# Image 0's key rotations on VectorE, and a different order of the work around the first projections, in a fused vision-transformer layer

## The chip, the cores and the metric

The kernel runs on one core of one Trainium2 chip. The metric is the device time of one launch in microseconds. Five engines work side by side, each on its own instruction list: TensorE (PE; its weight loads are shown apart as PEld), VectorE (DVE), ScalarE (ACT), GpSimd (POOL), and SyncE (SP), which issues the DMAs. They meet only at semaphores: an instruction waits for a count that others raise.

## The reference

32 images of 256x256 are filtered and then go through one transformer layer of 257 tokens (a class token and 256 rows) by 256 features. Cut to what matters:

```python
cur = img
for _ in range(3): cur, h, v, d = _dwt2(cur); details.append((h, v, d))
aw = sigmoid(cur.reshape(B, -1) @ Wa + ba)                  # one gate per image
w = softmax(flat(h, v, d) @ Wd + bd)                        # three gates per level and image
rec = idwt2(rec, h * w[0], v * w[1], d * w[2])              # rebuilt level by level
h = concat([cls_tok, rec])
h = h + attention(layernorm(h))     # 16 heads of 64, rotary q and k, alibi bias, causal
h = h + ffn(layernorm(h))           # ternary weights, 8-bit activations, silu gate
# rotary: q * cos + rotate_half(q) * sin, the same for k
# ternary: clip(round(w / mean|w|), -1, 1)
```

## The kernel before

**Start.** All images' gates are found first. TensorE multiplies the whole input by a map of ten bands (`zbank`, 128 products in four quarters `q`, one per landed quarter `xs[q]`), VectorE and ScalarE make softmax and sigmoid of the sums, TensorE spreads them to all partitions (`bcast_ready`), and VectorE turns them into small row operators, `image_operators(i, n)` for n images from i on. Meanwhile the feed-forward weights become ternary: `ternary(k, part)` on VectorE, three passes over 2048 columns for each of gate, up and down (k = 0, 1, 2; the "signs"); `turn_weights(w)` transposes them on TensorE (the "turnings"), and ScalarE copies each bank out (twice for each w). The quantiser's mean comes from one small product of TensorE ("mean product", into `psum[1]`).

**Each image a** then passes these stages. GpSimd makes its row operators (`row_operators`), TensorE filters it (`coarse`, `synthesise`), VectorE adds the parts (`image_out`) and takes the layernorm statistics (`image_stats`, `normalise_image`), TensorE transposes it (`turn_input`), ScalarE and VectorE split it into two fp16 halves (`input_hi`, `input_lo`). `project(b, g)`, g = 0 to 7, gives the queries (even g) and keys (odd g) two head pairs at a time in one PSUM bank; ScalarE's `to_rotate` copies each to `rq` (count `rq_ready`); SyncE moves it across partitions to `rot` by DMA (`rot_done`); GpSimd's `rotate(b, g)` multiplies `rq` by cos (`pcos_done`), `rot` by sin (`t2_ready`) and adds them (`qk_done`). Then come four value projections `project_v(b, v)` in the same bank, each read by ScalarE (`values_hi`) and VectorE (`values_lo`, count `vl_done`), and `project_v(b, v + 1)` waits for `values_lo(b, v)`. Then scores, softmax, output and the feed-forward part follow, interleaved with the next image.

**What sets the order** is the code itself. Every engine has a prologue written out by hand, and then a function `step(s)` run for every s from -4 on, which lists that engine's pieces for images s - 3 to s + 2; pieces whose image doesn't exist do nothing. Image 0's first pieces stand in the prologues. On GpSimd image 0's order is `add_bias(0)` (which adds the output bias `ob` and waits for VectorE's copy of it, `ob_copied`), rotations 0, 1 and 2, `row_operators(1)`, rotations 3, 4, 5, `image_rstd(1)`, rotations 6 and 7, `add_bias(1)`. On TensorE `project(0, 5)` stands behind the filtering of image 1. `out_bias` folds the class token's values into the output bias with float32 products, and `ob_ready` follows its last.

## Time and profile before

| | |
|---|---|
| median of 3 runs | 1754.96 us (1750.04 to 1756.24) |
| the profiled execution | 1752.32 us, its span 1750.5 us |
| busy share of the span | PE 95%, PEld 73%, DVE 84%, ACT 76%, POOL 64% |
| end of the start-up: `project_v(0, 3)` of image 0 done, its first scores | about 131 us |
| mean granted clock of TensorE | 0.976 of full speed |

The span is from the first to the last instruction. Busy shares are averages over the span; the change touches only the first 135 us of it, where TensorE is busy less (the profile's first three slices of 44 us show 7, 7 and 5 tenths). That stretch has to be read instruction by instruction.

### The profile page before, as it was taken

What the parts mean: (1) busy time and instruction counts of PE and PEld (TensorE: products, weight loads), DVE (VectorE), ACT (ScalarE), POOL (GpSimd) and SP (SyncE); (2) the same over time, 40 slices, a digit from 0 to 9 for tenths busy, and PEclk for the clock granted to TensorE, in tenths of its full rate; (3) what the DMA queues carried; (4) which work ended last, traced back from release to release, by engine and by line L of the source; (5) the groups of instructions that cost most, each with busy time, mean ns of one, the idle gap of its engine ahead of it and who ended that gap; (6) DMA issues with size and microseconds to landing.
All of it is one profiled execution on the core that took longest, in us unless ns stands there. A gap on an engine that the chain in (4) does not pass through costs nothing.

```text
span 1750.5 us, 48653 instructions
## 1 busy us (share of the span) xinstructions
PE 1664.2 (95%) x16742; PEld 1278.3 (73%) x16742; DVE 1470.0 (84%) x4972; ACT 1323.6 (76%) x3812; POOL 1120.1 (64%) x1034
## 2 busy tenths in 40 slices
PE   7758999999999999999999999999999999999975
PEld 6635777777777777777777777777777777777653
DVE  3837888899888888899888888899888888889874
ACT  0326888888888888888888888888888888888762
POOL 0087667766777666766777667666677667666500
PEclk9789999999999999999999999999999999999986
DMA  9311111111111111111111111111111111111100
GB/s 320 110 61 61 56 53 56 53 67 57 61 68 68 59 61 57 50 65 62 56 68 68 66 55 60 54 56 66 55 64 68 68 53 61 56 53 62 44 7 13
DMA packets 90168, 113.70 MB, mean 65 GB/s; under 512 B 14818, under 2 KB 52163, under 8 KB 89667
## 3 DMA queue, kind: packets, MB, share of 16 engines
q1 hardware_dynamic: 89922, 110.59, 18.1%
q8 instruction: 135, 2.21, 0.5%
q14 instruction: 111, 0.90, 0.2%
HBM read 26.62 MB, written 8.42 MB: 20 GB/s over the span
## 4 chain that ended last, share of the span: by engine, by line
PE 88%; DVE 4%; SPq 3%; POOL 2%; ACT 1%; issue 1%; DMA 0%; DVEq 0%; POOLq 0%; ACTq 0%
PE bank L725 45%; PE bank L842 9%; PE bank L983 7%; PE bank L831 6%; PE bank L829 6%; PE bank L994 3%; PE bank L853 3%; PE bank L903 3%; PE bank L891 2%; PE bank L1003 2%; SPq L320 1%; PE bank L882 1%; DVE arena L1283 1%; PE bank L950 0%; POOL rot L486 0%
## 5 line engine op out<-in xcount | busy, mean ns | idle before, releaser
L482 POOL TENSOR_TENSOR arena<-rq,cos 128x512 f32<-128x512 f32 x256 | 326.1, 1274 | 280.0 <-ACT rq L526 280.0
L535 ACT ACTIVATE arena<-arena,nm 128x129 f32<-128x129 f32 (+1 forms) x1024 | 455.6, 455 | 0.0
L486 POOL TENSOR_TENSOR rot<-rot,sin 128x512 f32<-128x512 f32 x256 | 326.3, 1275 | 103.9 <-DMA rot<-rq 103.9
L725 PE MATMUL bank<-xt_h,weights 128*128 128x256 f16 x2048 | 378.9, 273 | 9.2 <-ACT rq L526 7.8
L526 ACT ACTIVATE rq<-bank,bqk 128x256 f32<-128x256 f32 x512 | 214.4, 471 | 170.1 <-PE bank L725 155.3
L1283 DVE CUSTOM_DVE_ANT_0 arena<-bank,bias 128x129 f32<-128x129 f32 (+1 forms) x1024 | 317.9, 352 | 26.5 <-issue 16.6
L489 POOL TENSOR_TENSOR arena<-arena,rot 128x512 f32<-128x512 f32 x256 | 314.2, 1228 | 37.3 <-POOL rot L486 0.9
L1291 DVE TENSOR_TENSOR ptr_l<-bank,ptr_h 128x384 f16<-128x384 f32 x512 | 280.0, 552 | 31.8 <-ACT ptr_h L545 29.4
L545 ACT ACTIVATE ptr_h<-bank 128x384 f16<-128x384 f32 x512 | 249.1, 486 | 68.6 <-PE bank L725 44.0
L725 PE MATMUL bank<-xt_l,weights 128*128 128x256 f16 x1024 | 279.6, 273 | 0.0
L842 PE MATMUL bank<-eye,arena 128*128 128x128 f32 x1536 | 253.0, 277 | 8.5 <-DVE ptr_l L1291 4.4
L725 PEld LDWEIGHTS bank<-xt_h,weights 128*128 128x128 f16 x2048 | 200.5, 98 | 54.4 <-ACT rq L526 19.9
L842 PEld LDWEIGHTS bank<-eye,arena 128*128 128x128 f32 x1536 | 178.2, 141 | 43.8 <-issue 20.0
L535 ACT ACTIVATION_READ_ACCUMULATOR arena<-arena,nm 128x1 f32 x1024 | 203.9, 199 | 0.0
L725 PEld LDWEIGHTS bank<-arena,ptr_h 128*128 128x128 f16 x3072 | 175.7, 98 | 23.3 <-DVE ptr_l L1291 10.9
L725 PE MATMUL bank<-arena,ptr_h 128*128 128x64 f16 x3072 | 191.1, 193 | 0.1
L725 PE MATMUL bank<-arena,ptr_l 128*128 128x64 f16 x1536 | 178.9, 193 | 0.0
L725 PE MATMUL bank<-weights,arena 128*128 128x256 f16 x1536 | 178.5, 273 | 0.0
L725 PEld LDWEIGHTS bank<-weights,arena 128*128 128x128 f16 x1536 | 148.4, 98 | 16.6
L725 PE MATMUL bank<-weights,xt_h 128*128 128x512 f16 x512 | 152.7, 380 | 5.3 <-DVE arena L1404 4.2
L831 PE MATMUL bank<-arena 64*128 64x257 f32 x1024 | 155.1, 380 | 0.0
L983 PE MATMUL bank<-wgu,xqt 128*128 128x512 f16 x528 | 141.2, 390 | 5.1 <-ACT q2t L526 2.3
(200 smaller groups left out, 3182.5 us busy)
## 6 DMA issues: line engine op xcount, KB each, us to landing
rot<-rq SPq DMA_DIRECT2D x512, 128.0 KB, 2.0
arena<-in_x SPq DMA_DIRECT2D x4, 2048.0 KB, 15.2
xin<-in_x SPq DMA_DIRECT2D x32, 256.0 KB, 2.8
hr<-hr SPq DMA_DIRECT2D x32, 256.0 KB, 2.3
out<-h SPq DMA_DIRECT2D x64, 128.0 KB, 2.1
arena<-in_L_attn_w_qkv SPq DMA_DIRECT2D x2, 1536.0 KB, 8.6
weights<-in_L_ffn_w_down SPq DMA_DIRECT2D x1, 1024.0 KB, 11.8
arena<-in_L_ffn_w_gate SPq DMA_DIRECT2D x1, 1024.0 KB, 8.5
```

Of the source, the lines that this page charges most:

```text
L482: pool.tensor_tensor(dst, rq[:, g % 2].rearrange("p j (t n) -> p j t n", t=T), cos[:, :].rearrange("p (t n) -> p t n", t=T).unsqueeze(1).b ...
L486: pool.tensor_tensor(r, r, sin[:, :].unsqueeze(1).broadcast_to([P, 2, SIDE]), ALU.mult).then_inc(t2_ready, 1)
L489: pool.tensor_tensor(dst, dst, r.rearrange("p j (t n) -> p j t n", t=T), ALU.add).then_inc(qk_done, 1)
L526: return act.activation(dst, src, ACT.Identity, **kw)
L535: act.activation(cols, cols, ACT.Exp, bias=nm[:, t, h:h + 1], scale=-1.0, accum_out=rs[:, t, h:h + 1]).then_inc(e_done, 1)
L545: act.activation(ptr_h[:, h % PTR_RING], pt_bank[u % 2][:, 0:3 * P].rearrange("p (b n) -> p b n", b=3), ACT.Copy).then_inc(hi_done, 1)
L725: ins = pe.matmul(dst, lhs[l], rhs[r], start=start and n == 0, stop=stop and n == len(parts) - 1)
L831: pe.matmul(bank[:, W0:SCOLS], qt[par][half, j, P:SIDE], kt[par][half, j, :], start=True, stop=True).then_inc(s_ready, 1)
L842: ins = pe.transpose(pt_bank[u % 2][:, n * P:(n + 1) * P], r[:, col:col + P], eye[:, :])
L983: ins = pe.matmul(bank[:, :], xqt[:, kc, t * P:(t + 1) * P], wgu[:, kc, base + half * 512:base + (half + 1) * 512], start=kc == 0, stop=kc ...
L1283: dve.tensor_tensor_reduce(r[:, cols], bank[:, cols], b, -1.0, 3.0e38, ALU.add, ALU.min, nm[:, t, h:h + 1]).then_inc(t_done, 1)
L1291: tt(ptr_l[:, h % PTR_RING], pt_bank[u % 2][:, 0:3 * P].rearrange("p (b n) -> p b n", b=3), ptr_h[:, h % PTR_RING], ALU.subtract).then_inc ...
```

## The change

In words, engine by engine, all before the steady state:

- **TensorE**: the mean product moves from behind quarter 2 of the band sums into quarter 3, behind its 25th of 32 products. The turnings move: gate from before the class token's products to behind them, up behind `project(0, 1)`, down behind `project(0, 2)`. All of `out_bias` stands behind `project(0, 0)`, where half stood ahead of it. Its banks for the turnings are 0, 1, 4, 6 where they were 0 to 3.
- **VectorE**: only two of nine sign passes stay ahead of the band sums' reduction; the up pass 2 goes behind `normalise_image(0)`, and the three down passes behind the class token's columns. `image_operators(1, 16)` moves from ahead of `input_lo(0)` to behind `rotate(0, 1)` and the copy of `ob`. Rotations 1, 3, 5 and 7 of image 0 (the keys) are new on VectorE; between them stand `image_out(1)`, `image_stats(1)` and the split of the output weights (`wo_l`); `image_operators(17, 15)` comes behind the last.
- **GpSimd**: keeps rotations 0, 2, 4, 6 of image 0, and `rotate(0, 0)` comes ahead of `add_bias(0)`. The two engines count the same semaphores, so each rotation waits for the one before it at each of its three instructions.
- **ScalarE**: the six copies of the turned weights and the copy of the output weights (`wo_h`) are spread between `coarse_out(0)`, `input_hi(0)` and `to_rotate` 0 to 3.
- **SyncE**: `move(0)`, whose target `hr2` now holds the down signs for longer, waits for all turnings too.

The diff, cut to its core:

```diff
@@ GpSimd
             def rotate(b, g):
-                if not image(b):
+                if not image(b) or begun and (b, g) == (0, 0) or b == 0 and g % 2:
                     return
                 pool.wait_ge(rq_ready, 8 * b + g + 1)
+                if b == 0 and g:
+                    pool.wait_ge(pcos_done, g)
...
+                if b == 0 and g:
+                    pool.wait_ge(t2_ready, g)
...
+                if b == 0 and g:
+                    pool.wait_ge(qk_done, g)
...
             pool.wait_ge(late_in, 16 * 13)
+            image_rstd(0)
+            rotate(0, 0)
+            begun = True
@@ ScalarE
+            coarse_out(0)
+            weights_out(0)
+            weights_out(1)
+            input_hi(0)
+            to_rotate(0, 0)
+            to_rotate(0, 1)
+            weights_out(2)
+            weights_out(3)
+            to_rotate(0, 2)
+            weights_out(4)
+            weights_out(5)
             act.wait_ge(rawo_in, 16)
             act.wait_ge(tern_ready, 3)
             act.activation(wo_h[:, :, :], rawo, ACT.Copy, scale=WSCALE).then_inc(w_hi, 1)
@@ TensorE
             synthesise(0)
             coarse(0)
-            pe.wait_ge(turned_copied, 4)
             cls_part(psum[3], (2,), range(PAIRS))
+            pe.wait_ge(mean_ready, 1)
+            turn_weights(0)
             turn_input(0)
...
-            out_bias(range(0, 4))
             project(0, 0)
-            out_bias(range(4, PAIRS))
+            out_bias(range(PAIRS))
             pe.matmul(psum[2][:, 0:SIDE], ones[0:1, :], bo_row, start=False, stop=True).then_inc(ob_ready, 1)
+            project(0, 1)
+            turn_weights(1)
+            project(0, 2)
+            turn_weights(2)
@@ VectorE
+            def rotate(b, g):
+
+                r = rot[:, g % 2].rearrange("p j (t n) -> p j t n", t=T)
+                dst = rope_out(b % 2, GROUPS[g])
+                dve.wait_ge(rq_ready, g + 1)
+                dve.wait_ge(pcos_done, g)
+                tt(dst, rq[:, g % 2].rearrange("p j (t n) -> p j t n", t=T),
+                   cos[:, :].rearrange("p (t n) -> p t n", t=T).unsqueeze(1).broadcast_to([P, 2, T, P]), ALU.mult).then_inc(pcos_done, 1)
+                dve.wait_ge(rot_done[g % 2], 32 * (g // 2 + 1))
+                dve.wait_ge(t2_ready, g)
+                tt(rot[:, g % 2], rot[:, g % 2], sin[:, :].unsqueeze(1).broadcast_to([P, 2, SIDE]), ALU.mult).then_inc(t2_ready, 1)
+                dve.wait_ge(pcos_done, g + 1)
+                dve.wait_ge(t2_ready, g + 1)
+                dve.wait_ge(qk_done, g)
+                tt(dst, dst, r, ALU.add).then_inc(qk_done, 1)
...
             normalise_image(0)
-            dve.wait_ge(ops_ready, 1)
-            image_operators(1, 16)
+            ternary(1, 2)
             input_lo(0)
...
+            for part in range(3):
+                ternary(2, part)
+            prep_chain.settle()
+            rotate(0, 1)
             dve.wait_ge(ob_ready, 1)
-            prep_chain.settle()
             dve.tensor_copy(ob[:, :], psum[2][:, 0:SIDE]).then_inc(ob_copied, 1)
+            dve.wait_ge(ops_ready, 1)
+            image_operators(1, 16)
+            rotate(0, 3)
+            image_out(1)
+            image_stats(1)
+            rotate(0, 5)
+            dve.wait_ge(w_hi, 11)
+            stt(wo_l[:, :, :], rawo, WSCALE, wo_h[:, :, :], ALU.mult, ALU.subtract).then_inc(wo_split, 1)
+            rotate(0, 7)
             dve.wait_ge(ops_ready, 2)
             image_operators(17, 15)
```

The instruction order shows two places that matter. The first is VectorE from the last piece of `input_lo(0)` to the first `values_lo` (`arena<-bank,arena` with a wait for `vh_done`). Before, from the weights' split on:

```order
L1192 SCALAR_TENSOR_TENSOR weights<-arena,weights 128x1024 [waits w_hi] x2
L1471 SCALAR_TENSOR_TENSOR weights<-arena,weights 128x2048 [waits w_hi]
L1474 COPY gs<-magic 128x1 [waits w_split,prep]
L1477 COPY arena<-bqk 128x8 [waits cls_turned_in]
L1477 COPY arena<-bqk 128x8
L1480 COPY ob<-bank 128x256 [waits prep,ob_ready]
L1171 TENSOR_TENSOR arena<-fac,pats 128x1440 [waits ops_ready]
L1174 TENSOR_REDUCE ops<-arena 128x480 [waits prep]
L1413 TENSOR_TENSOR hh<-bank,pair_sum 128x512 [waits coarse_out_done,hr_ready,syn_ready,ob_copied]
L1322 BN_STATS st<-hh 128x6 [waits h_ready]
L1322 BN_STATS st<-hh 128x6
```

After the change, the end of the same stretch, from `image_out(1)` (`hh<-bank,pair_sum`) to the first `values_lo`:

```order
L1372 TENSOR_SCALAR ve<-mv 128x2 [waits chain_a]
L1354 TENSOR_TENSOR arena<-rq,cos 128x2x2x128 [waits pcos_done,rq_ready]
L1358 TENSOR_TENSOR rot<-rot,sin 128x512 [waits t2_ready,rot_done1]
L1362 TENSOR_TENSOR arena<-arena,rot 128x2x2x128 [waits qk_done,t2_ready,pcos_done]
L1532 SCALAR_TENSOR_TENSOR weights<-arena,weights 128x2048 [waits w_hi]
L1354 TENSOR_TENSOR arena<-rq,cos 128x2x2x128 [waits pcos_done,rq_ready]
L1358 TENSOR_TENSOR rot<-rot,sin 128x512 [waits t2_ready,rot_done1]
L1362 TENSOR_TENSOR arena<-arena,rot 128x2x2x128 [waits qk_done,t2_ready,pcos_done]
L1200 TENSOR_TENSOR arena<-fac,pats 128x1440 [waits ops_ready]
L1203 TENSOR_REDUCE ops<-arena 128x480 [waits prep]
L1448 SCALAR_TENSOR_TENSOR arena<-bank,arena 128x512 [waits vh_done,ob_copied]
L1448 SCALAR_TENSOR_TENSOR arena<-bank,arena 128x512 [waits vh_done] x2
```

Ahead of `values_lo(0, 0)` there are now two of the key rotations (six `TENSOR_TENSOR`, 5 and 7), the output weights' split (`weights<-arena,weights` of 2048 columns) and `image_operators(17, 15)` (the pair of 1440 and 480 columns). Before, all but the rotations were done ahead of `image_out(1)`.

The second is GpSimd from the scale of image 0's layernorm (`rstd`) to `row_operators(1)`. Before:

```order
L472 TENSOR_TENSOR rstd<-ve,negh 128x2 [waits var_ready,late_in]
L500 TENSOR_TENSOR hr<-hh,ob 128x512 [waits h_ready,ob_copied]
L482 TENSOR_TENSOR arena<-rq,cos 128x512 [waits rq_ready]
L486 TENSOR_TENSOR rot<-rot,sin 128x512 [waits rot_done0]
L489 TENSOR_TENSOR arena<-arena,rot 128x512 [waits t2_ready,pcos_done]
L482 TENSOR_TENSOR arena<-rq,cos 128x2x2x128 [waits rq_ready]
L486 TENSOR_TENSOR rot<-rot,sin 128x512 [waits rot_done1]
L489 TENSOR_TENSOR arena<-arena,rot 128x2x2x128 [waits t2_ready,pcos_done]
L482 TENSOR_TENSOR arena<-rq,cos 128x512 [waits rq_ready]
L486 TENSOR_TENSOR rot<-rot,sin 128x512 [waits rot_done0]
L489 TENSOR_TENSOR arena<-arena,rot 128x512 [waits t2_ready,pcos_done]
L451 COPY op_now<-ops 128x32 [waits coarse_ready,syn_ready,ops_ready]
```

After the change:

```order
L476 TENSOR_TENSOR rstd<-ve,negh 128x2 [waits var_ready,late_in]
L488 TENSOR_TENSOR arena<-rq,cos 128x512 [waits rq_ready]
L494 TENSOR_TENSOR rot<-rot,sin 128x512 [waits rot_done0]
L499 TENSOR_TENSOR arena<-arena,rot 128x512 [waits t2_ready,pcos_done]
L510 TENSOR_TENSOR hr<-hh,ob 128x512 [waits h_ready,ob_copied]
L488 TENSOR_TENSOR arena<-rq,cos 128x512 [waits pcos_done,rq_ready]
L494 TENSOR_TENSOR rot<-rot,sin 128x512 [waits t2_ready,rot_done0]
L499 TENSOR_TENSOR arena<-arena,rot 128x512 [waits qk_done,t2_ready,pcos_done]
L453 COPY op_now<-ops 128x32 [waits coarse_ready,syn_ready,ops_ready]
L455 TENSOR_TENSOR s<-xin 128x256 [waits x_in]
L457 TENSOR_TENSOR rowop<-op_now,avg 128x512 [waits coeffs]
L460 TENSOR_TENSOR s<-s 128x128
```

One rotation instead of three stands between `add_bias(0)` (`hr<-hh,ob`) and `row_operators(1)` (from `op_now` on), and one has gone ahead of `add_bias(0)`; the second has new waits for what VectorE does in between.

## Rows read from the trace of the kernel before

**Rows 1.** The page's head: span, and busy time by engine.

```profile
span 1750.5 us, 48653 instructions
PE 1664.2 (95%) x16742; PEld 1278.3 (73%) x16742; DVE 1470.0 (84%) x4972; ACT 1323.6 (76%) x3812; POOL 1120.1 (64%) x1034
```

**Rows 2.** The chain that ended last, 0 to 140 us: start us, us, what.

```profile
58.97 4.18 DMA sin<-table_sin
...
72.13 1.82 PE bank L787 x16
...
109.23 2.93 PE bank L903 x6
...
113.97 1.50 PE bank L725 x12
...
120.32 0.85 ACT rq L526 x2
...
123.43 0.70 DVE arena L1404
...
137.22 0.48 ACT rq L526
137.84 0.47 SPq L367
138.35 2.03 DMA rot<-rq
```

**Rows 3.** Timeline of POOL, 92 to 132 us: start, us, instruction [idle before].

```profile
92.28 2.61 POOL L500 TENSOR_TENSOR hr<-hh,ob 128x512 f32<-128x512 f32 x1 [10.54 <-DVE ob L1480]
94.85 1.26 POOL L482 TENSOR_TENSOR arena<-rq,cos 128x512 f32<-128x512 f32 x1
...
106.34 0.21 POOL L451 COPY op_now<-ops 128x32 f32<-128x32 f32 x1
...
108.88 0.29 POOL L460 TENSOR_TENSOR s<-s 128x64 f32<-128x64 f32 x1
...
130.57 1.32 POOL L500 TENSOR_TENSOR hr<-hh,ob 128x512 f32<-128x512 f32 x1
```

**Rows 4.** Timeline of DVE, 63 to 148 us.

```profile
63.76 1.20 DVE L1182 TENSOR_SCALAR weights<-weights 128x2048 f32<-128x2048 f32 x1
...
82.43 1.75 DVE L1171 TENSOR_TENSOR arena<-fac,pats 128x1536 f32<-128x1536 f32 x1
...
89.16 2.29 DVE L1471 SCALAR_TENSOR_TENSOR weights<-arena,weights 128x2048 f16<-128x2048 f32 x1
...
91.77 0.43 DVE L1480 COPY ob<-bank 128x256 f32<-128x256 f32 x1
92.11 1.65 DVE L1171 TENSOR_TENSOR arena<-fac,pats 128x1440 f32<-128x1440 f32 x1
93.80 1.83 DVE L1174 TENSOR_REDUCE ops<-arena 128x480 f32<-128x1440 f32 x1
...
129.80 2.24 DVE L1428 TENSOR_SCALAR xn<-hh,mv,rstd 128x256 f32<-128x256 f32 x2
...
147.01 2.87 DVE L1379 TENSOR_TENSOR h<-h,ob 128x256 f32<-128x256 f32 x2
```

**Rows 5.** Timeline of PE, `out_bias`, in two halves of 8 passes.

```profile
83.48 3.62 PE L803 MATMUL bank<-arena,hr 128*128 128x256 f32 x8
...
88.99 1.89 PE L803 MATMUL bank<-arena,hr 128*128 128x256 f32 x8
```

**Rows 6.** Timeline of ACT, 67 to 85 us.

```profile
67.39 3.71 ACT L646 ACTIVATE wgu<-bank 128x1024 f16<-128x1024 f16 x4
...
74.96 1.91 ACT L652 ACTIVATE weights<-arena 128x2048 f16<-128x2048 f32 x1
...
83.72 0.84 ACT L526 ACTIVATE xt_h<-bank,neg_cls 128x256 f16<-128x256 f32 x2 [5.01 <-PE bank L882]
```

**Rows 7.** Busy time per 1 us stretch: PE, PEld, DVE, ACT, POOL, PEclk, DMA share, GB/s.

```profile
102.00:103.00 1.00, 0.69 (x4) 0.18 (x2) 0.00 (x0) 0.00 (x0) 1.00 (x2) 0.51 0.00 0
110.00:111.00 1.00, 1.00 (x4) 0.82 (x3) 0.00 (x0) 0.00 (x0) 1.00 (x2) 0.50 0.00 0
```

More of the change, by code:

```diff
@@ L372, in move @@
                 sp.wait_ge(hr_ready, c + 1)
+                if c == 0:
+                    sp.wait_ge(turned, 6)
                 fence(sp)
@@ L468, in image_rstd @@
             def image_rstd(a):
-                if not image(a):
+                if not image(a) or begun and a == 0:
                     return
@@ L556, in input_hi @@
             def input_hi(a):
-                if not image(a):
+                if not image(a) or begun and a == 0:
                     return
@@ L576, in tokens_out @@
                 identity(xqt[:, :, :].rearrange("p k n -> p (k n)"), u_bank[:, 0:SIDE].bitcast(F16), bias=half_zero[:, 0:1]).then_inc(xqt_done, 1)
+            begun = False
             def to_rotate(b, g):
-                if not image(b):
+                if not image(b) or begun and b == 0 and g < 3:
                     return
@@ L599, in coarse_out @@
             def coarse_out(a):
-                if not image(a):
+                if not image(a) or begun and a == 0:
                     return
@@ L641, in _, with weights_out @@
                     act.activation(ez[0:IMAGES, :], zz[0:IMAGES, :], ACT.Exp).then_inc(ez_ready, 1)
-            for u in range(6):
+            def weights_out(u):
                 act.wait_ge(turned, u + 1)
-                src = psum[u % 4][:, :].bitcast(F16)
+                src = psum[(0, 1, 4, 6)[u % 4]][:, :].bitcast(F16)
                 if u < 4:
@@ L652, in _ @@
             act.activation(wo_h[:, :, :], rawo, ACT.Copy, scale=WSCALE).then_inc(w_hi, 1)
+            begun = True
             def step(s):
@@ L906, in project @@
             def project(b, g):
-                if not image(b) or begun and (b, g) == (0, 0):
+                if not image(b) or begun and b == 0 and g < 3:
                     return
@@ L1239, in _ @@
             mark(tt(wsc[:, 12:13], wsc[:, 9:10], wsc[:, 10:11], ALU.mult))
-            for k in range(2):
-                for part in range(3):
-                    ternary(k, part)
+            ternary(0, 0)
+            ternary(0, 1)
             dve.wait_ge(z_done, 4)
@@ L1406, in image_out @@
             def image_out(a):
-                if not image(a) or begun and a == 0:
+                if not image(a) or begun and a < 2:
                     return
@@ L1416, in image_stats @@
             def image_stats(a):
-                if not image(a) or begun and a == 0:
+                if not image(a) or begun and a < 2:
                     return
```

23 lines of the change are left out of this document (9 added, 14 removed).

## The prediction

> **What bounds the kernel now.** I read the page's head first: TensorE is busy for 95% of 1750.5 us [rows 1], and from about 150 us on nothing is changed. So the question is by how much the first 135 us grow or shrink, since everything after them follows image 0 and image 1 at TensorE's pace. Then the chain of work that ended last, in order of time. Up to 63.15 us (58.97 + 4.18) it runs over SyncE's queue and ends with the last sine table's DMA [rows 2], for which the softmax waits. From there TensorE, VectorE and GpSimd take turns. The reader is to see three stretches in it. First, up to image 0's first projection, which follows on the first half of `out_bias` at 83.48 + 3.62 = 87.1 us [rows 5]. Second, GpSimd: it gets `ob` at 92.2 us and needs until 109.2 us for `add_bias(0)`, three rotations (94.85 to 106.34, so 3.83 us each) and `row_operators(1)` (106.34 to 109.17, 2.8 us) [rows 3]; TensorE's filtering of image 1 starts at 109.23 [rows 2]. Third, a round trip per projection: from 113.97 us on TensorE waits for ScalarE's copy each time, the last copy ends at 120.32 + 0.85 = 121.2 us, and `values_lo(0, 0)` starts at 123.43 [rows 2]. GpSimd's rotations 3 to 7 run until 130.57 us [rows 3] beside that, in step with it. The landmark of my sum is the start of `values_lo(0, 0)`, 123.43 us: behind it all engines have the same work in the same order in both kernels.
>
> **The band sums, up to the softmax: nothing.** The mean product no longer stops TensorE between the quarters, so the sums end some 6 us sooner, and the first sign passes start about 1 us later. The cover is the sine table's DMA at 63.15 us, whose queue isn't touched. VectorE now idles there, since it has only three sign passes ahead of it. The other six, at 1.2 us each [rows 4], come later; this is the price of the head start.
>
> **Up to `project(0, 0)`: 2.7 us sooner.** The down turning, 1.82 us, leaves TensorE's way to the filtering of image 0 [rows 2]. Against it, TensorE has stood nearly idle since 61 us, so I charge 0.4 us for the spreading product at the low clock. That leaves 1.4 us. Half of `out_bias`, 3.62 us [rows 5], and `image_operators(1, 16)`, 1.75 + 1.9 us [rows 4], leave the way as well, but what shows next is ScalarE: two copies of turned weights (3.71 / 4 = 0.93 us each [rows 6]) now stand ahead of `input_hi(0)`, which ended at 84.56 us [rows 6]. I let it end at 83.4, `input_lo(0)` at 84.2, and `project(0, 0)` start at 84.4 instead of 87.1 us. Bounds: 83.9, and 85.4 if the gate turning runs at the low clock.
>
> **Up to `ob_copied`: 7 us later.** This is what GpSimd waits for. TensorE: the projection at the low clock takes 2.5 us, to 86.9. Then come 18 passes (16 and the bias row's two), 0.45 us each at the low clock and 0.24 at the full one (3.62 / 8 and 1.89 / 8 [rows 5]); with 4 low and 14 full that is 5.2 us, to 92.1 us. `project(0, 1)` takes 1.5 us and its copy 0.85 [rows 2]: `rq_ready` 2 at 94.6 us. The move across partitions takes 2.7 us from the copy's end to its landing (137.70 to 140.38 us in image 1 [rows 2]): 97.3 us. VectorE stands in `rotate(0, 1)` for it, and behind it in VectorE's list stand the copy of `ob` and `image_operators(1, 16)`. No row shows a 128x512 rotation instruction on VectorE. The nearest are the float32 products of 1440 columns in 1.65 us and 1536 in 1.75 us [rows 4], 1.04 ns a column, so 0.6 to 0.7 us. Sine and sum take it to 98.7, the copy of `ob` (0.43 us [rows 4]) to 99.2 us, against 92.2. GpSimd, done with `rotate(0, 0)` by 95, has nothing to do until then.
>
> **`row_operators(1)`: 1.3 us later.** `add_bias(0)` takes 2.61 us, as before, beside `image_operators` (it takes 1.32 us alone [rows 3]): to 101.9. One rotation, 3.83, and `row_operators(1)`, 2.8, give 108.6 us. To that comes the price of two engines at once. The same 1.3 us of GpSimd are seen doubled when a VectorE product of 1.65 us runs beside them [rows 3, 4], two VectorE sums of 256 columns took 2.87 us beside rotations where 0.3 us each is expected from the 1.04 ns, and the layernorm's two passes took 2.24 us [rows 4] beside a rotation's end. So they don't share, they take turns, and each pays for the other. `rotate(0, 3)` on VectorE falls right beside `rotate(0, 2)` and the operators on GpSimd: three instructions, 1.9 us more, 110.5 us against 109.2. Bound below: without this turn-taking GpSimd ends at 107.2 us.
>
> The Trainium skill ("SBUF — State Buffer", section "Who interferes with whom") says that a VectorE instruction with two SBUF inputs and a GpSimd instruction that reads SBUF lock each other out for their full length. By that rule, the rows agree, and it speaks against the point of this change: rotations on both engines at once cost their sum.
>
> **SyncE.** `move(0)` stands ahead of `rotate(0, 3)`'s DMAs in its queue and now waits for `add_bias(0)` at 101.9 us; ScalarE's `rq_ready` 4 comes at about 101.9 too, because the last weight copies and `wo_h` (1.91 us [rows 6]) stand ahead of `to_rotate(0, 3)`. One issue, 0.5 us [rows 2], is hidden behind the turn-taking.
>
> **To the landmark: 10.7 us later.** From the filtering on the path is as before (109.23 to 113.97, and on to 121.2 us [rows 2]), shifted by 1.3: `rq_ready` 6 at 117.6, 7 at 120.1 and 8 at 122.5 us. On VectorE, in its order: `rotate(0, 5)` gets its moved half at 120.3, is held by GpSimd's cosine of rotation 6 until 121.3, and ends at 122.6. The split of the output weights takes 2.29 us [rows 4]: 124.9. `rotate(0, 7)` now meets GpSimd's sine and sum of rotation 6 and `add_bias(1)`, which waited for the split: 1.9 us of its own and 3.8 of theirs give 130.6 us. `image_operators(17, 15)` takes 1.65 + 1.83 us [rows 4]: 134.1 us. Only then comes `values_lo(0, 0)`, long after its values are there, and `project_v(0, 1)` waits for it. That is 134.1 - 123.4 = 10.7 us.
>
> **The clock: 1 us.** TensorE stands idle for those 10 us. After a wait near 100 us the granted clock fell to 0.50, 1.2 GHz, and was still there at 110 us after a longer wait [rows 7]. `project_v(0, 1)`, six products at half speed, costs about 1.3 us more; between 0 and 2.6 us, I take 1.
>
> **Sum.** 10.7 + 1 = 11.7 us. The profiled execution took 1752.32 us (span 1750.5), the median of the runs is 2.6 us above it. On the one it gives 1764.0, on the other 1766.7 us; I say 1765. Own bounds. Below, no turn-taking: row operators at 107.2, `rq_ready` 8 at 119.2, its move landed at 121.9, sine and sum to 123.3, operators to 126.8 us, 3.4 us late; on the profiled execution 1756, on the median 1758 us. Above: all 18 passes at the low clock (3 us) and two value projections too (1.6 us): 16 us, 1769 to 1771 us.
>
> **The rivals.** A measurement of this kernel can tell about 0.5%, 8.8 us, from no change.
>
> - *Forecast, 0.62: the engines take turns and the tail on VectorE holds the values up*, 1762 to 1770 us, slower.
> - *The engines overlap freely, 0.20.* For it: the multiplications of the rotation have never been seen on VectorE, and the rows of turn-taking are few. Then the delay is 3.4 to 6 us, 1756 to 1760, within 0.5%.
> - *The tail is hidden later, 0.12.* GpSimd and ScalarE come out of the start-up with less queued, and image 1's stage has waits that might take up a few us of it; 1755 to 1759 us. Against it: image 1's work begins with TensorE's projections and everything behind them shifts alike.
> - *The load is shared as it looks on paper, 0.06, faster.* GpSimd is rid of four rotations of 3.83 us between 92 and 131 us. If it bounds all of that stretch, and if VectorE is through with `image_operators(17, 15)` within 2.3 us of `rq_ready` 8 (123.43 - 121.2, the point from which this decides), what counts is the one rotation less ahead of `row_operators(1)` and the head start of 2.7 us at `project(0, 0)`: 3.8 + 2.7 = 6.5 us, 1746 to 1749 us; with more of the four rotations on the path, 1743. Against it: from 113.97 us on the trips between TensorE and ScalarE set the pace, and VectorE's order puts 3.5 us of operators behind a rotation that can't end sooner than 4 us after that copy.
>
> **How the numbers follow.** 1765 is the likeliest case. The range takes it in, reaches down to the free overlap and up to the low clock's bound: 1757 to 1770 us. Above 8.8 us lies the forecast's case less a part of its lower edge, and a little of the others: slower 0.64. Within 0.5%: overlap, hiding, and that edge, 0.31. Faster by over 0.5% needs more than one rotation's gain: 0.05.
>
> **What the profile of the changed kernel would show.** The first `rq` copy at about 87 us instead of 89.2. GpSimd idle between about 95 and 99 us, with VectorE's copy of `ob` as what ends it. VectorE's rotation instructions, 0.6 to 0.7 us alone, and over 1 us or GpSimd's over 1.8 us where both run. Filtering of image 1 at 110.5 us. A long wait of TensorE's `project_v(0, 1)` (about 10 us, ended by VectorE's `values_lo`) is the decisive line; if it is under 4 us, the tail didn't happen and the prediction falls. If `ob_copied` comes by 96 us, or rotations on both engines keep their own lengths, the steps before it are wrong.

## The result and the profile after

The changed kernel takes 1767.36 us (median; 1766.95 to 1769.03) where the kernel before takes 1752.9. The ratio is 1.0084 with a 95% interval of 1.0069 to 1.0099: slower, and by more than the 0.5% that the prediction asks for. The forecast was added to an earlier median of the kernel before, 1754.96 us of three executions. Single executions far above the rest (one of experiment 7 at 4266.9 us, two of the kernel before at 1938.4 and 2817.8 us) are left out of every ratio. The profiled execution took 1769.03 us against 1752.32, and its span grew by 16.7 us. The page's head, which answers to [rows 1]:

```profile
span 1767.2 us, 48668 instructions
PE 1673.1 (95%) x16742; PEld 1281.0 (72%) x16742; DVE 1482.6 (84%) x4984; ACT 1323.5 (75%) x3812; POOL 1109.1 (63%) x1022
```

GpSimd has lost its four rotations (12 instructions), and its busy time fell by only 11.0 us, less than 4 times 3.83. VectorE gained the same twelve and 12.6 us. TensorE runs the same 16742 products and is busy for 8.9 us more, at a mean granted clock of 0.967 instead of 0.976: a slower clock, not more work.

The chain that ended last shows where the time went (start us, us, what; compare [rows 2]):

```profile
112.13 0.30 POOL s L462
...
112.47 2.93 PE bank L928 x6
...
117.89 2.75 PE bank L754 x12
...
121.57 2.75 PE bank L754 x12
...
128.02 0.85 ACT rq L539 x2
...
129.52 2.05 DMA rot<-rq
...
131.59 1.13 DVE rot L1358
...
132.80 1.58 DVE arena L1362
134.38 1.58 DVE arena L1200
...
137.71 0.69 DVE arena L1448
...
138.44 2.76 PE bank L754 x6
...
149.64 0.44 PE bank L907 x2
```

Read the first column against [rows 2]. Filtering of image 1 starts at 112.47 us, where it was 109.23 (+3.2). It and `image_out(1)` take 5.4 us to `project(0, 5)`, where it was 4.74 (+0.7). A `project` lasts 2.75 us where it was 1.50; three of them add 3.8, and the last copy to `rq` stands at 128.02 instead of 120.32 us. `values_lo(0, 0)` comes 8.8 us behind the end of that copy, where it was 2.3 (+6.6). That makes 14.3 us at the landmark: 137.71 against 123.43. Two value projections at 2.76 us follow, and image 1's `turn_input` starts at 149.64 us. From ScalarE's first `xt_h` of image 1, behind it, to the end of the span nearly the same is left in every kernel here: 1617.0 us before, 1616.9 after, 1614 to 1618 in the experiments. So that start is the second landmark: 133.52 us before, 150.34 after.

TensorE's wait that the prediction called decisive is there, 6.72 us long where about 10 were forecast (its timeline: start, us, instruction, idle before and what ended it):

```profile
138.44 1.04 PE L754 MATMUL bank<-weights,xt_h 128*128 128x512 f16 x2 [6.72 <-DVE arena L1448]
```

VectorE's timeline in the same execution, with `rotate(0, 1)`, the copy of `ob`, `image_operators(1, 16)`, the first instruction of `rotate(0, 3)`, the split of the output weights and the start of `rotate(0, 7)`:

```profile
96.29 0.69 DVE L1354 TENSOR_TENSOR arena<-rq,cos 128x512 f32<-128x512 f32 x1 [3.79 <-ACT rq L539]
100.14 0.69 DVE L1358 TENSOR_TENSOR rot<-rot,sin 128x512 f32<-128x512 f32 x1 [3.16 <-DMA rot<-rq]
100.92 0.69 DVE L1362 TENSOR_TENSOR arena<-arena,rot 128x512 f32<-128x512 f32 x1
101.53 0.42 DVE L1524 COPY ob<-bank 128x256 f32<-128x256 f32 x1
101.86 1.75 DVE L1200 TENSOR_TENSOR arena<-fac,pats 128x1536 f32<-128x1536 f32 x1
...
106.06 1.67 DVE L1354 TENSOR_TENSOR arena<-rq,cos 128x512 f32<-128x512 f32 x1 [0.49 <-POOL arena L488]
...
127.09 2.28 DVE L1532 SCALAR_TENSOR_TENSOR weights<-arena,weights 128x2048 f16<-128x2048 f32 x1
129.29 1.75 DVE L1354 TENSOR_TENSOR arena<-rq,cos 128x512 f32<-128x512 f32 x1
```

A rotation instruction takes 0.69 us while GpSimd is idle, and between 1.09 and 1.75 us beside a GpSimd one. GpSimd's side of it (its timeline; compare [rows 3]):

```profile
102.03 2.71 POOL L510 TENSOR_TENSOR hr<-hh,ob 128x512 f32<-128x512 f32 x1 [7.00 <-DVE ob L1524]
...
108.80 0.67 POOL L453 COPY op_now<-ops 128x32 f32<-128x32 f32 x1
...
110.11 1.58 POOL L457 TENSOR_TENSOR rowop<-op_now,avg 128x512 f32<-128x512 f32 x1
```

It waited 7 us for `ob`, and the copy that took 0.21 us before takes 0.67 beside VectorE's rotation.

The last view is the clock. Busy time in stretches of 5 us, in the order PE, PEld, DVE, ACT, POOL, then TensorE's granted clock (compare [rows 7]):

```profile
105.00:110.00 5.00, 0.00 (x0) 0.00 (x0) 4.04 (x4) 0.84 (x2) 4.87 (x5) 0.84 0.28 105
...
115.00:120.00 5.00, 4.21 (x14) 1.93 (x13) 1.86 (x6) 0.38 (x1) 1.95 (x2) 0.50 0.16 52
120.00:125.00 5.00, 3.38 (x15) 1.79 (x13) 0.89 (x2) 1.50 (x4) 0.00 (x0) 0.50 0.15 54
...
140.00:145.00 5.00, 3.58 (x9) 0.89 (x7) 0.69 (x1) 0.60 (x1) 0.00 (x0) 0.50 0.00 0
```

In the kernel before, the same columns read:

```profile
110.00:115.00 5.00, 4.16 (x18) 2.77 (x17) 1.60 (x5) 0.38 (x1) 4.86 (x5) 0.77 0.12 30
115.00:120.00 5.00, 3.14 (x28) 2.34 (x26) 0.34 (x3) 1.68 (x4) 3.10 (x4) 1.00 0.21 77
```

Before, TensorE stood idle for 6.5 us ahead of the filtering of image 1; the clock came back during the filtering, and projections 5 to 7 ran at 2.4 GHz. In this execution after the change it stood idle for 7.8 us ahead of the filtering, and its clock stayed at 1.2 GHz through filtering, projections and the first value projection until 132 us; it then rose and fell again within the wait for `values_lo`. Experiments 2, 3 and 6 below show that this is not how the clock must go after such an idle time.

### The profile page after: what moved, and what is told of

Read it like the earlier page. It is cut to its first block, busy times and chain, and to the rows that moved or that the text cites. A ratio compares the mean times of both kernels' runs of the same rounds, so it can differ in the third digit from the quotient of the medians.

```text
span 1767.2 us, 48668 instructions
## 1 busy us (share of the span) xinstructions
PE 1673.1 (95%) x16742; PEld 1281.0 (72%) x16742; DVE 1482.6 (84%) x4984; ACT 1323.5 (75%) x3812; POOL 1109.1 (63%) x1022
## 4 chain that ended last, share of the span: by engine, by line
PE 87%; DVE 3%; ACT 1%; POOL 1%; issue 1%; DMA 0%; SPq 0%; DVEq 0%; POOLq 0%; ACTq 0%
PE bank L754 45%; PE bank L867 9%; PE bank L1008 7%; PE bank L856 6%; PE bank L854 6%; PE bank L1019 3%; PE bank L878 3%; PE bank L928 2%; PE bank L916 2%; PE bank L1028 2%; PE bank L907 1%; DVE arena L1311 0%; PE bank L975 0%; DVE es L1496 0%; DVE ptr_l L1319 0%
## 5 line engine op out<-in xcount | busy, mean ns | idle before, releaser
L488 POOL TENSOR_TENSOR arena<-rq,cos 128x512 f32<-128x512 f32 x252 | 321.5, 1276 | 309.1 <-ACT rq L539 309.1
L754 PE MATMUL bank<-xt_h,weights 128*128 128x256 f16 x2048 | 382.9, 275 | 9.2 <-ACT rq L539 5.9
L494 POOL TENSOR_TENSOR rot<-rot,sin 128x512 f32<-128x512 f32 x252 | 322.2, 1279 | 103.4 <-DMA rot<-rq 103.3
L499 POOL TENSOR_TENSOR arena<-arena,rot 128x512 f32<-128x512 f32 x252 | 309.6, 1229 | 37.0 <-POOL rot L494 1.3
## 6 DMA issues: line engine op xcount, KB each, us to landing
rot<-rq SPq DMA_DIRECT2D x512, 128.0 KB, 2.0
out<-h SPq DMA_DIRECT2D x64, 128.0 KB, 2.1
```

The costliest lines, as they stand in the source:

```text
L488: pool.tensor_tensor(dst, rq[:, g % 2].rearrange("p j (t n) -> p j t n", t=T), cos[:, :].rearrange("p (t n) -> p t n", t=T).unsqueeze(1).b ...
L494: pool.tensor_tensor(r, r, sin[:, :].unsqueeze(1).broadcast_to([P, 2, SIDE]), ALU.mult).then_inc(t2_ready, 1)
L499: pool.tensor_tensor(dst, dst, r.rearrange("p j (t n) -> p j t n", t=T), ALU.add).then_inc(qk_done, 1)
L754: ins = pe.matmul(dst, lhs[l], rhs[r], start=start and n == 0, stop=stop and n == len(parts) - 1)
```

## The experiments

Ten kernels, each timed in turns with the kernel before, whose median lay between 1752.9 and 1753.5 us in these comparisons; each ratio is to the executions beside it. "Landmarks" are the start of VectorE's copy of `ob`, the end of `row_operators(1)`, the start of the last copy to `rq`, of `values_lo(0, 0)` and of image 1's `xt_h`, all us of the profiled execution. Two executions differ by up to 2.3 us in them from the start on, since the last sine table lands at another time (VectorE's `zz` at 62.6 to 65.0 us); the medians even that out over several runs.

| kernel | `ob` | row ops | last `rq` | `values_lo` | `xt_h` | median us | ratio to before (95%) |
|---|---|---|---|---|---|---|---|
| before | 91.8 | 109.2 | 120.3 | 123.4 | 133.5 | 1752.9 | |
| after | 101.5 | 112.4 | 128.0 | 137.7 | 150.3 | 1767.4 | 1.0084 (1.0069 to 1.0099) |
| 1 no sharing | 93.1 | 109.1 | 121.6 | 125.5 | 138.1 | 1751.9 | 0.9998 (0.9984 to 1.0012) |
| 2 tail forward | 101.1 | 115.3 | 127.0 | 133.9 | 147.8 | 1767.6 | 1.0077 (1.0059 to 1.0094) |
| 3 `ob` first | 91.8 | 106.6 | 118.4 | 130.0 | 143.9 | 1762.2 | 1.0047 (1.0029 to 1.0064) |
| 4 TensorE kept busy | 100.6 | 111.5 | 121.1 | 132.9 | 146.9 | 1766.0 | 1.0070 (1.0052 to 1.0088) |
| 5 tables in PSUM | 100.3 | 110.5 | 123.5 | 134.1 | 148.0 | 1764.7 | 1.0071 (1.0055 to 1.0087) |
| 6 values first | 99.5 | 110.4 | 122.2 | 125.3 | 139.9 | 1756.6 | 1.0029 (1.0016 to 1.0041) |
| 7 both, 3 and 6 | 91.8 | 106.5 | 118.4 | 121.5 | 133.5 | 1753.2 | 1.0004 (0.9995 to 1.0013) |
| 8 sharing alone | 89.6 | 105.7 | 116.9 | 123.2 | 137.1 | 1757.6 | 1.0027 (1.0017 to 1.0037) |
| 9 operators later | 93.5 | 108.0 | 119.8 | 122.9 | 133.7 | 1751.2 | 0.9992 (0.9980 to 1.0003) |
| 10 two rotations | 92.7 | 107.5 | 119.3 | 122.5 | 132.6 | 1749.0 | 0.9982 (0.9973 to 0.9992) |

**1. Everything but the sharing.** All eight rotations go back to GpSimd, without the extra waits; the rest of the change stays.

```diff
-                if not image(b) or begun and (b, g) == (0, 0) or b == 0 and g % 2:
+                if not image(b) or begun and (b, g) == (0, 0):
...
-            rotate(0, 1)
...
-            rotate(0, 3)
...
-            rotate(0, 5)
...
-            rotate(0, 7)
```

> Only the sharing is undone: GpSimd rotates all eight groups of image 0 (rotation 0 still ahead of the bias addition), VectorE none; the rest of the change stays. The prediction's theory (VectorE's rotations hold up the copy of ob by 7 us, the operators by turns with GpSimd, and the values by a tail of 6 to 9 us): the copy of ob at about 94.5 us, image 1's filtering from about 108 to 109 us, the first values_lo at 2.3 us behind the last rq copy (123 to 124 us), 1750 to 1754 us, as before the change. Rival (the reordering of signs, turnings and out_bias costs the time, not the sharing): filtering of image 1 not before 111 us and 1760 us or more.

Measured: level with before. Without the sharing the whole loss of 15 us is gone; the spread signs, turnings and mean product gain and lose nothing that can be told by themselves. (That the sharing costs less in the old order is experiment 8.) In the row, `values_lo` is 2 us later than before and `xt_h` 4.6, with the value projections at 1.2 GHz; that execution was 3.5 us above the one of before, while the medians agree. The time of an execution goes with its mean granted clock: the three of the ten at 0.969 to 0.970, the profiled one among them, took 1755.8 to 1757.0 us, the seven at 0.974 to 0.978 took 1749.0 to 1753.8. So a single execution can't settle differences of this size.

**2. The tail taken forward.** The split of the output weights and `image_operators(17, 15)` go ahead of `image_out(1)`.

```diff
             rotate(0, 3)
+            dve.wait_ge(w_hi, 11)
+            stt(wo_l[:, :, :], rawo, WSCALE, wo_h[:, :, :], ALU.mult, ALU.subtract).then_inc(wo_split, 1)
+            dve.wait_ge(ops_ready, 2)
+            image_operators(17, 15)
             image_out(1)
```

> The sharing stays; the split of the output weights (2.3 us) and image_operators(17, 15) (3.5 us) go ahead of image_out(1), where VectorE waited 6.6 us. Prediction's theory (the tail behind rotation 7 holds the values): the wait of TensorE's second value projection, 6.7 us, falls to about 1 to 3 us, values_lo about 5 us sooner, 1761 to 1763 us. Rival (the tail is cover for something else, such as rotation 7 itself, its move and GpSimd's turn): the time falls by under 2 us.

A miss: nothing gained. GpSimd's timeline, the last two sums of the row operators (0.39 and 0.29 us in the changed kernel):

```profile
111.20 2.44 POOL L460 TENSOR_TENSOR s<-s 128x128 f32<-128x128 f32 x1
113.72 1.59 POOL L462 TENSOR_TENSOR s<-s 128x64 f32<-128x64 f32 x1
```

VectorE's split stood beside them from 110.05 for 3.34 us (2.28 alone), and its product from 113.31 for 1.85. The row operators ended 2.9 us later than in the changed kernel. The tail, from the last copy's end to `values_lo(0, 0)`, became 2.8 us shorter (6.0 us instead of 8.8), so the two cancel, as the medians do (1767.56 against 1767.36). In this execution `values_lo(0, 0)` still came 3.9 us and `xt_h` 2.6 us sooner, but for another reason: TensorE's clock came back during the filtering, although TensorE had been idle for 10.5 us ahead of it and nothing of its list was changed (stretches as above):

```profile
115.00:120.00 5.00, 4.51 (x8) 2.52 (x8) 2.07 (x3) 0.38 (x1) 4.02 (x4) 0.54 0.00 0
120.00:125.00 5.00, 2.97 (x24) 2.19 (x24) 2.46 (x7) 1.25 (x4) 0.69 (x1) 1.00 0.23 80
```

From the end of the row operators to the start of the last copy to `rq` it took 11.7 us here and 11.8 in experiments 3 and 6, against 15.6 in the profiled execution of the changed kernel and 11.1 before. Work moved out of a tail must not land beside the other engine's path.

**3. The copy of `ob` first.** It and `image_operators(1, 16)` stand ahead of `rotate(0, 1)`.

```diff
-            rotate(0, 1)
             dve.wait_ge(ob_ready, 1)
             dve.tensor_copy(ob[:, :], psum[2][:, 0:SIDE]).then_inc(ob_copied, 1)
             dve.wait_ge(ops_ready, 1)
             image_operators(1, 16)
+            rotate(0, 1)
             rotate(0, 3)
```

> The copy of ob and image_operators(1, 16) go ahead of rotation 1 on VectorE. Prediction's theory (GpSimd idles 7 us behind VectorE's wait for the moved half): GpSimd's bias addition at about 94.5 instead of 102 us, row operators of image 1 at 105 to 107 instead of 112.4 us, and the whole 5 to 7 us sooner, 1760 to 1762 us, more if TensorE's clock then stays up. Rival (GpSimd needs rotation 1 anyway, since rotation 2 waits for VectorE's part): row operators not before 110 us, gain under 3 us.

As expected, 5 us less, at the upper end of 1760 to 1762 us. From the start of the copy of `ob` to the end of the row operators it takes 14.8 us; in experiment 1, which differs there by rotation 1 on GpSimd, 16.1. So a rotation of 3.83 us taken off GpSimd is worth 1.3 us. But `values_lo(0, 0)` still comes 10.8 us behind that copy's end, and `xt_h` is 10.4 us later than before the change.

**4. TensorE kept busy ahead of the filtering.** 64 products into a free bank, whose results nobody reads.

```diff
+                if a == 1:
+                    pe.wait_ge(turned_copied, 3)
+                    for _ in range(64):
+                        pe.matmul(o_bank[:, 0:SIDE], eye16[:, :], xt_h[:, 0, :], start=True, stop=True)
                 pe.wait_ge(rowop_ready, a + 1)
```

> 64 extra fp16 products of 128x256 on TensorE into a bank that nobody reads then, ahead of image 1's coarse part, where TensorE waited 7.8 us for GpSimd; nothing else is changed. Theory of the clock (the idle stretch brings TensorE down to 1.2 GHz and it stays there over projections 5 to 7 and three value projections): granted clock 1.00 over the stretch, projections 5 to 7 take 1.5 instead of 2.75 us, 4 to 6 us less in all, 1761 to 1764 us. Rival (the projections' length is hidden behind VectorE's tail, so the clock costs nothing): projections shorter but values_lo not over 1 us sooner.

Half a miss. The busy stretches show the clock at its full level through the projections, and lost again behind them:

```profile
115.00:120.00 5.00, 3.14 (x28) 2.33 (x27) 1.63 (x6) 1.68 (x4) 1.42 (x3) 1.00 0.32 108
120.00:125.00 5.00, 2.56 (x17) 1.26 (x14) 4.04 (x4) 1.44 (x3) 3.58 (x2) 1.00 0.29 108
125.00:130.00 5.00, 0.00 (x0) 0.00 (x0) 4.91 (x4) 0.00 (x0) 3.87 (x3) 0.57 0.00 0
```

Projections 5 to 7 took 2.42 us a round trip, and the last `rq` copy came at 121.1 instead of 128.0 us. Of those 6.9 us, 4.8 were left at `values_lo` (VectorE's tail is a chain of its own), and 3.5 at `xt_h`, since all three value projections behind the wait were now at 1.2 GHz. The median gained 1.4 us, less than the 4 to 6 expected. The low clock at the projections and the tail on VectorE partly cover each other. How much of the 6.9 us is the products' doing is not shown by this pair alone: from the end of the row operators to the last copy it took 9.6 us here, which is 2.2 us less than in experiments 3 and 6, where the clock came back without them.

**5. The tables in PSUM.** VectorE copies cos and sin once into an idle bank and reads them there, so that its two products have one operand in SBUF instead of two.

```diff
+            mark(dve.tensor_copy(psum[3][:, 0:SIDE], cos[:, :]))
+            mark(dve.tensor_copy(psum[3][:, SIDE:512], sin[:, :]))
...
-                   cos[:, :].rearrange("p (t n) -> p t n", t=T).unsqueeze(1).broadcast_to([P, 2, T, P]), ALU.mult).then_inc(pcos_done, 1)
+                   psum[3][:, 0:SIDE].rearrange("p (t n) -> p t n", t=T).unsqueeze(1).broadcast_to([P, 2, T, P]), ALU.mult).then_inc(pcos_done, 1)
```

> The changed kernel, with a copy of the cosine and sine tables in an idle PSUM bank (two copies of 256 columns, 0.6 us on VectorE), from which VectorE's rotations read them; so two of the three instructions of a key rotation have one SBUF input. Theory of turn-taking (two SBUF inputs beside GpSimd's reads): those instructions keep 0.7 us beside a busy GpSimd (1.67, 1.29, 1.75, 1.12 us before), and GpSimd's beside them 1.25; only the sum still meets it. Row operators of image 1 about 1 us sooner, the tail behind rotation 7 about 2 us shorter, 1764 to 1766 us. Rival (the length comes from the DMA or from waiting for semaphores): lengths as in the changed kernel, time unchanged or 0.6 us more.

The lengths are as expected, the tail is not. VectorE's timeline for `rotate(0, 3)`, at the same place beside GpSimd's rotation 2:

```profile
104.84 0.69 DVE L1354 TENSOR_TENSOR arena<-rq,bank 128x512 f32<-128x512 f32 x1 [0.48 <-POOL arena L488]
106.89 0.69 DVE L1358 TENSOR_TENSOR rot<-rot,bank 128x512 f32<-128x512 f32 x1 [1.37 <-DMA rot<-rq]
107.67 0.95 DVE L1362 TENSOR_TENSOR arena<-arena,rot 128x512 f32<-128x512 f32 x1
```

The two with the table in PSUM take 0.69 us each where they took 1.67 and 1.29; the sum, whose inputs both still lie in SBUF, takes 0.95. GpSimd's `op_now` copy is back at 0.21 us. So it is where the operands lie, not the mere company, that makes them take turns. The Trainium skill ("SBUF — State Buffer", section "Who interferes with whom") says that a VectorE instruction with at most one SBUF input, outside its two-port modes, doesn't contend with GpSimd. This pair of runs agrees: 0.69 us beside a busy GpSimd. The median is 2.6 us lower, but the trace doesn't tie all of that to the turn-taking. From the end of the copy of `ob` to the end of the row operators it took 9.7 us instead of 10.5, and rotation 7 took 4.4 us instead of 5.1. The tail from the last copy's end was 9.7 us, longer than the 8.8 us before, where some 2 us less were expected; and the clock, which came back one projection into the three, also brought the last copy forward.

**6. The values first.** The split waits until the row operators are done and stands ahead of `image_out(1)`; `values_lo(0, 0)` stands inside rotation 7, and the two instructions of `image_operators(17, 15)` behind it, ahead of `values_lo` 1 and 2.

```diff
             rotate(0, 3)
+            dve.wait_ge(rowop_ready, 2)
             dve.wait_ge(w_hi, 11)
             stt(wo_l[:, :, :], rawo, WSCALE, wo_h[:, :, :], ALU.mult, ALU.subtract).then_inc(wo_split, 1)
...
+                if g == 7:
+                    values_lo(0, 0)
                 dve.wait_ge(rot_done[g % 2], 32 * (g // 2 + 1))
```

> The changed kernel, with the tail taken out of the values' way without a collision: the output weights' split waits for image 1's row operators and then runs ahead of image_out(1); values_lo(0, 0) stands between cosine and sine of rotation 7; image_operators(17, 15) in two pieces between the values. Theory of the tail: values_lo(0, 0) at 2.3 us behind the last rq copy instead of 8.8, TensorE's wait for it under 2 us, its clock higher; 6 to 9 us less, 1758 to 1762 us. Rival (as moving the tail forward gained nothing in the time, something behind it sets the end): under 3 us less.

It gained 10.8 us, more than expected: `values_lo(0, 0)` again comes 2.3 us behind the last copy's end, as before the change, and the clock is 1.00 from 115 to 130 us. Behind that it falls once more (0.70 and 0.61 in the next two stretches of 5 us), and `xt_h` is 6.4 us later than before the change.

**7. Experiments 3 and 6 together.**

> Both repairs: ob and image_operators(1, 16) ahead of rotation 1, and the values ahead of the tail. If the two are the whole loss: row operators at 106.5 us, last rq copy done at 119.3, first values_lo at 121.6, the start-up 1 to 2 us shorter than before the change, 1749 to 1753 us, a ratio of 0.998 to 1.000. Rival (turn-taking and the clock keep a part of the loss): 1755 to 1758 us.

Level with before, just above the 1749 to 1753 us expected, and a ratio of 1.0004 where 1.000 was the upper end. Up to `values_lo(0, 0)` it leads the kernel before by 1.9 us; at `xt_h` the lead is gone (133.51 against 133.52), because `values_lo(0, 1)` stands behind rotation 7's sum and a product (VectorE's timeline):

```profile
123.23 1.58 DVE L1367 TENSOR_TENSOR arena<-arena,rot 128x512 f32<-128x512 f32 x1
124.74 1.65 DVE L1201 TENSOR_TENSOR arena<-fac,pats 128x1440 f32<-128x1440 f32 x1
126.31 0.68 DVE L1460 SCALAR_TENSOR_TENSOR arena<-bank,arena 128x512 f16<-128x512 f32 x1
```

**8. The sharing alone**, put into the kernel before. The `rotate` functions of both engines are those of the change; VectorE's list gets

```diff
             image_operators(17, 15)
             dve.wait_ge(ob_copied, 1)
+            rotate(0, 1)
+            rotate(0, 3)
+            image_out(1)
+            image_stats(1)
+            rotate(0, 5)
+            rotate(0, 7)
             begun = True
```

> The kernel before the change, with its own order of signs, turnings, out_bias and operators; only the sharing is done, VectorE rotating image 0's keys behind image_operators(17, 15), with image_out(1) and image_stats(1) between. Theory (sharing costs because VectorE's list holds ob, the operators and the split behind a rotation's wait; alone, with these done, it is harmless): row operators of image 1 at 105 to 107.5 us instead of 109.2, the first values_lo 4 to 5 us behind the last rq copy instead of 2.3, so 1750 to 1755 us, the same within 0.2%. Rival (turn-taking alone costs several us wherever the rotations stand): 1758 us or more.

A miss, 0.27% or 4.7 us slower, between what the theory (up to 1755 us) and its rival (1758 or more) gave, although all that stood ahead of `image_out(1)` is still ahead of the rotations. From the copy of `ob` to the end of the row operators it takes 16.2 us (89.55 to 105.7) where the kernel before takes 17.4: again a rotation less on GpSimd is worth 1.2 us, and the rest of the 3.4 us by which its row operators are sooner was there at the copy of `ob`. Then `values_lo(0, 0)` waits for rotation 7 (VectorE's timeline),

```profile
120.65 1.00 DVE L1336 TENSOR_TENSOR rot<-rot,sin 128x512 f32<-128x512 f32 x1 [2.07 <-DMA rot<-rq]
121.74 1.58 DVE L1340 TENSOR_TENSOR arena<-arena,rot 128x512 f32<-128x512 f32 x1
123.24 0.68 DVE L1426 SCALAR_TENSOR_TENSOR arena<-bank,arena 128x512 f16<-128x512 f32 x1
```

5.5 us behind the last copy's end instead of 2.3, and TensorE, idle meanwhile, comes back at 1.2 GHz, as ScalarE's copies of the values show by their idle times:

```profile
126.75 0.60 ACT L603 ACTIVATE arena<-bank 128x512 f16<-128x512 f32 x1 [6.79 <-PE bank L731]
130.90 0.60 ACT L603 ACTIVATE arena<-bank 128x512 f16<-128x512 f32 x1 [3.56 <-PE bank L731]
135.06 0.60 ACT L603 ACTIVATE arena<-bank 128x512 f16<-128x512 f32 x1 [3.56 <-PE bank L731]
```

At 2.4 GHz the idle time between two of them is 2.29 us. From `values_lo(0, 0)` to `xt_h` it takes 13.9 us instead of 10.1: three times 1.27 is 3.8 us that a wait of 3.2 us brought with it. So of the 15 us of the change somewhat under 5 are the sharing in the old order; the other 10 need the new order too, which puts the copy of `ob`, the operators and the split behind rotations.

**9. The operators one value later** than in 7: the product ahead of `values_lo(0, 2)`, the reduction ahead of `values_lo(0, 3)`.

> The run before last in this direction (copy of ob first, values_lo(0, 0) inside rotation 7) was level with the kernel before: its lead of 2 us at values_lo(0, 0) (121.49 against 123.43 us) was gone at values_lo(0, 1), which stood behind rotation 7's sine and sum and the product of image_operators(17, 15). Here the product stands behind values_lo(0, 1) and its reduction behind values_lo(0, 2). Theory: the values then follow at TensorE's pace, 2.9 us apart or less; values_lo(0, 1) at 124.4 us, image 1's first xt_h at about 131.6 us (before 133.52), 1750 to 1752 us, ratio 0.998 to 0.9995. Rival: rotation 7's sine, which waits for its DMA and for GpSimd's sine of rotation 6, holds values_lo(0, 1) by itself; then nothing is gained on that run, 1753 us, and VectorE's list shows an idle time ahead of that sine and values_lo(0, 1) after 126 us.

The rival's place was right: `values_lo(0, 1)` comes at 126.42 us, straight behind rotation 7's sum (124.91, 1.58 us); the idle time it foretold ahead of the sine isn't there, only 1.40 us ahead of `values_lo(0, 0)`. `xt_h` at 133.7 is 2 us later than the theory had it. The time, 1751.24 us, lies where the theory put it, but its interval holds 1; whether it is better than 7 stays open.

**10. Only rotations 1 and 3 on VectorE.** The copy of `ob` first as in 3, the split behind the row operators as in 6, `image_operators(17, 15)` behind `image_stats(1)`.

```diff
-                if not image(b) or begun and (b, g) == (0, 0) or b == 0 and g % 2:
+                if not image(b) or begun and (b, g) == (0, 0) or b == 0 and g in (1, 3):
...
             image_stats(1)
-            rotate(0, 5)
...
-            rotate(0, 7)
             dve.wait_ge(ops_ready, 2)
             image_operators(17, 15)
```

> VectorE takes only the rotations 1 and 3, which stand ahead of the row operators on the path; 5 and 7 are GpSimd's again. The copy of ob and image_operators(1, 16) come first, the split of the output weights waits for the row operators, and image_operators(17, 15) follows image_stats(1). Theory: the loss sits in what VectorE must do behind rotation 5, the gain in the row operators' being 3 us sooner. So: row operators done at about 106.5 us, last copy to rq at 118.4 to 119.2 us, values_lo(0, 0) at 121.5 us without a long wait ahead of project_v(0, 1), TensorE's clock full from about 115 us, first xt_h of image 1 at 131.5 to 132 us (before 133.52): 1750 to 1752 us, ratio 0.998 to 0.9995. Rival: GpSimd, with two engines' reads of the same tables and five rotations behind the row operators, falls back so far that the copies to rq wait for their buffers, or the clock stays low past 120 us as in the changed kernel: then xt_h at 133.5 us or later, 1753 us or more.

The fastest of all, and below the 1750 to 1752 us expected: 1749.0 us, 18 below the changed kernel and 0.18%, some 3 us, below the one before (0.9973 to 0.9992). That is less than the 0.5% by which this document calls a kernel faster, though the interval leaves out 1. VectorE waits for the values again, and not they for it, and they follow at full clock:

```profile
122.51 0.69 DVE L1448 SCALAR_TENSOR_TENSOR arena<-bank,arena 128x512 f16<-128x512 f32 x1 [4.80 <-ACT arena L612]
125.39 0.69 DVE L1448 SCALAR_TENSOR_TENSOR arena<-bank,arena 128x512 f16<-128x512 f32 x1 [2.19 <-ACT arena L612]
```

Of the gain only 0.9 us shows at `xt_h`. The span behind `xt_h` was 1614.4 and 1614.8 us in 9 and 10 against 1617.0 before; no experiment looked for what shortened it. The granted clock tells a part: of the 22 executions of the kernel before that were timed beside it, eight ran at 0.968 to 0.973 and took 1754.0 us or more, and of the twelve of experiment 10 only one was at 0.973 (1751.2 us). Without these the medians are 1750.7 and 1748.9 us, so about half of the gain is that executions at the lower clock hardly occur here.

## Why the prediction was right, and where it was off

1765 us was forecast, 1767.4 measured, inside 1757 to 1770, and the mechanism held: engines that take turns, and a tail on VectorE that holds the values (experiments 5 and 6). That the sum came so near was partly luck, since its errors have both signs. By its own steps:

- **The band sums: nothing gained.** Held: VectorE idles 5 us ahead of the softmax, whose sine table landed 1 us later in this execution.
- **`project(0, 0)` 2.7 us sooner.** It started at 85.5 us instead of 84.4, so 1.6 us sooner; the missing 1.1 us is of the size of that landing.
- **`ob_copied` 7 us later.** Right in kind, too small in size: the copy started at 101.53, 9.8 us later than before. Of the 2.8 us beyond the forecast, 1.6 were there when ScalarE's copy for `rotate(0, 1)` ended (96.2, forecast 94.6 us), and 1.2 came in its move across partitions (3.9 us until VectorE's sine starts, forecast 2.7). The instructions themselves took what was forecast, 0.69 us each. Experiment 3 takes the wait away and gains 5 us.
- **`row_operators(1)` 1.3 us later.** Measured 3.2: the delay of `ob` passed on, while from the end of its copy it took 10.5 us, forecast 11.3. That there is turn-taking in it is shown by experiment 5, where this stretch is 0.7 us shorter; the forecast charged 1.9 us for it. The 1.32 us that the forecast read as `add_bias` alone stood beside VectorE's two layernorm passes (129.80 us, 2.24 us), so that row didn't show GpSimd by itself.
- **The tail.** 8.8 us from the last copy's end to `values_lo(0, 0)`, where the forecast had 11.6 (122.5 to 134.1). That copy came so late that the split of the weights ended 0.5 us behind it and not 2.4; rotation 7 then took 5.1 us (forecast 5.7) and the operators 3.4 (3.5). Experiment 6 shows it as the largest part: 10.8 us once the values don't stand behind it, clock included.
- **The clock: 1 us.** This is the term that was furthest off in the profiled execution. The forecast let projections 5 to 7 run as before ("the path is as before", "shifted by 1.3"), and charged the low clock to one value projection. Measured were 0.7 us up to `project(0, 5)`, 3.8 in the projections, and 2.6 in two value projections: 7 us. The 2.6 us stand behind a long wait, as in experiments 3, 4 and 8, where three value projections ran at 1.2 GHz (experiment 1 had two slow ones although no wait there was over 2.0 us, so a long wait isn't needed). The 0.7 us are found in experiments 2, 3 and 6 as well, where the same stretch took 5.3 to 5.4 us. The 3.8 us are not: in those three TensorE was idle for 10.5, 3.2 and 6.8 us ahead of the filtering, and projections 5 to 7 then ran at 2.4 GHz, as the forecast had it. So they don't follow from the change alone. Whether the projections were slow in the other three executions of the changed kernel too, 1766.95 to 1767.38 us, no trace shows, and how much of the 3.8 us is in the median stays open. Experiment 4 shows besides that time won at the projections doesn't all reach `xt_h`.

So the sum for the profiled execution was 5 us short (1764.0 forecast, 1769.0 measured): 6 us of clock and 1.9 at the row operators too little, 2.8 of tail too much. The medians are 14.5 us apart and the two profiled executions 16.7, where 11.7 was forecast; the forecast for the median, 1765 to 1766.7, looks better than its terms because it was added to 1754.96 us and not to 1752.9.

That the load is shared as it looks on paper (0.06) can now be priced. One rotation less on GpSimd ahead of the row operators is 1.2 or 1.3 us (experiments 8 and 3), not 3.83. With `ob` and the values out of the rotations' way, sharing four rotations is level with before (7), and sharing only two gains 3 us (10), still inside 0.5%.

## What to carry to other kernels

Before work is moved to an idle engine, read what stands behind it in that engine's list, and who waits for that: here a copy of 0.4 us and a subtraction of 0.7 us, each queued behind a rotation that waited for its DMA, cost more than the four moved rotations could bring. Ask of both engines whether their operands lie in SBUF: if so, side by side is nearly one after the other. And price a new wait of TensorE with the slow products behind it, which in experiment 8 doubled a wait of 3 us. Don't charge what the clock does in one trace to a change before kernels with the same list for TensorE have been seen: here they differ by 3.8 us.

## What the runs showed of the hardware that was not expected

- How little company it takes: beside VectorE's split (3.34 us) and the product behind it two GpSimd sums of 0.39 and 0.29 us took 2.44 and 1.59 us; the first ended 0.25 us behind the split (experiment 2).
- How long the low clock lasts. After an idle 7.8 us it stayed at 0.50 in the changed kernel over filtering, three projections and a value projection, until 132 us. Before the change it rose to 1.00 during the same filtering after an idle 6.5 us, and in experiment 2 after an idle 10.5 us. What decides between them these runs leave open.
- The start of an execution varies by up to 2.3 us with the landing of one small table, in kernels that don't touch its queue.
